# The f16 halves of x go through a DMA transpose, and GpSimd's constant-operand copies become tensor-scalar operations

## The chip, the cores and the metric

One core of a Trainium2 chip runs the kernel. The metric is the device time of one execution in microseconds (us); lower is better. Engines are named as the profile names them: PE is TensorE's matmul side and PEld its weight loads, DVE is VectorE, ACT is ScalarE, POOL is GpSimd, SP is SyncE, whose instruction queue issues nearly all DMA transfers here (SPq in the profile).

## What is computed

A decoder layer over 32 sequences of 128 tokens with 256 channels, 16 heads of width 16: linear attention with random features, cross attention, a ternary gated feed-forward; a layer norm stands behind each. Cut to its core:

```python
q, k, v = (split(x @ W.T + b) for W, b in ((Wq, bq), (Wk, bk), (Wv, bv)))
q_phi, k_phi = phi(q), phi(k)          # phi(y) = exp(y @ orf.T / dk**.25 - |y|^2 / (2 dk**.5)) + eps
kv = einsum('bhlm,bhld->bhmd', k_phi, v)
att = einsum('bhlm,bhmd->bhld', q_phi, kv) / einsum('bhlm,bhm->bhl', q_phi, k_phi.sum(2))[..., None]
x = layernorm(x + merge(att) @ Wo.T + bo)
s = softmax((x_heads @ xWq.T) @ (ctx_heads @ xWk.T).T / 4) @ (ctx_heads @ xWv.T)
x = layernorm(x + merge(s))
h = silu(quant(x) @ tern(w_gate).T) * (quant(x) @ tern(w_up).T)
out = layernorm(x + quant(h) @ tern(w_down).T)
```

In the cross attention x gives the queries, the context keys and values. `quant` rounds to 8-bit levels per token, `tern` rounds weights to -1, 0, 1.

## The kernel before

One tile is one sequence: 128 tokens on the partitions, 256 channels along them. A tile's work is cut into some 110 named steps, and all engines run a software pipeline written out by hand: each engine has a function `iteration(i, par)` that lists its steps in a fixed order, and `go(step, i, par, lag)` runs the step on tile i - lag. So in iteration i TensorE projects tile i - 1, makes features of tile i - 3, scores of tile i - 6, the feed-forward of tiles i - 8 and i - 9. Iterations 0 to 13 are written out, 14 to 31 are a loop of two iterations a pass, and 32 to 41 are written out again and drain the pipeline. Each step raises a semaphore (`done[name]`, for transposes by DMA `moved[name][par]`), and `wait(eng, name, t, off)` waits for it. An engine does its steps in order, so a waiting step holds all behind it.

Around the change:

- x of a tile is loaded by SP (`load_x`, L286) into `xs`. POOL makes its f16 half `xhi` (L394) by a multiplication with a tensor of ones, and the rest `xlo` (L401), both into the single buffer `xpk`.
- `xTp` (L1070) on TensorE transposes `xpk` in 4 blocks of 128x128 into bank 6, late in iteration t, between `st0` and `st1`. `xT_` (L539) on ScalarE copies them to `xT`, as the last step of its iteration. `qkm` (L1088) in iteration t + 1 reads `xT` first, right behind `s0`; `vm` reads it again later.
- SP's list in an iteration (L338) is `load_c`, `load_x`, `cT_`, `kT`, `hqT_`, `qT`, `row`, `tT_`, `load_r`, `store`. `cT_`, `kT`, `hqT_`, `qT` and `tT_` are DMA transposes of [128, 1024] in f16 or bf16, all issued at L305 and waited for in `wait_ahead` (L242). `tT_` waits for `tlo` of DVE (L857), `row` for `mT` of ACT (L612), `hqT_` for `hq0` of POOL, `kT` for `lo` of POOL.
- The hidden layer comes quantised through `hs` (DVE) - `hm1`, `hm0` (ACT) - `hq1`, `hq0` (POOL, L469 to L477, an addition of a broadcast constant) - `hqT_` (SP, DMA) - `dn` (TensorE, L1293). Behind `dn` in TensorE's list stand `vm`, `tm`, `kvp`, `wo`, `st0`.
- `tm` (L1177) - `thi` (ACT, L602) - `tlo` (DVE) - `tT_` (SP): the query side of the scores. DVE does `kvm_` and `ad3` ahead of `tlo`.
- POOL's other operations with a constant operand: `chi` (L449, context, 512 elements a partition), `xqf` (L463, 256).

Of the kernel before, what the change touches and what calls it, by code (L numbers as in the profile page):

```python
# [12 lines left out]
P = 128  # L13
# [17 lines left out]
def decoder_kernel(nc: bass.Bass, x, ctx_in, Wq, bq, Wk, bk, Wv, bv, Wo, bo, orf,  # L31
# [4 lines left out]
    with ExitStack() as stack:  # L36
# [6 lines left out]
        def sem(name):  # L43
# [54 lines left out]
        xT = sb("xT", [P, 4, P], F16)  # L98
# [96 lines left out]
        at_xT = pb[6][:, 0:256]  # L195
# [30 lines left out]
        moved = {name: [sem(f"s_{name}{i}") for i in range(2)] for name in ("qT", "kT", "cT", "tT", "hqT", "row")}  # L226
# [15 lines left out]
        def wait_ahead(eng, t, *producers):  # L242


            counts = [t + off + 1 for _, off in producers]
            counts = [v if isinstance(v, int) else eng.to_reg(v) for v in counts]
            eng.wait_ge(ids, 3)
            for (name, _), v in zip(producers, counts):
                if not isinstance(v, int) or v > 0:
                    eng.wait_ge(done[name], v)  # L250
# [27 lines left out]
        def _(sp):  # L278
# [27 lines left out]

            def qT(t, par):

                wait_ahead(sp, t, ("phq0", -1))
                transpose(pkAT[:, 0:PAIRS, :], pkA[:, 0:PAIRS, :, :].rearrange("p c r d -> p (c r d)"), "qT", par)  # L310
# [27 lines left out]
            def iteration(i, par):  # L338
                go(load_c, i, par, 4)
                go(load_x, i, par, 0)  # L340
                go(cT_, i, par, 5)
                go(kT, i, par, 2)
                go(hqT_, i, par, 9)
                go(qT, i, par, 2)
                go(row, i, par, 6)
                go(tT_, i, par, 5)
                go(load_r, i, par, 3)
                go(store, i, par, 10)
# [6 lines left out]
        def _(pool):  # L355
# [38 lines left out]
            def xhi(t, par):  # L394

                landed(pool, x_in, t, par)
                wait(pool, "xTp", t, -1)
                g.tensor_tensor(xpk[:, 0, :], xs[:, par, :], onesf[:, 0:1].to_broadcast([P, D]),
                                ALU.mult).then_inc(done["xhi"], 1)
# [49 lines left out]
            def chi(t, par):  # L449

                landed(pool, c_in, t, par)
                wait_moved(pool, "cT", t, par, -1)
                c3 = cs[:, par, :].rearrange("p (h d) -> p h d", h=H)
                g.tensor_tensor(pkC[:, :, 0:2, :], c3.unsqueeze(2).to_broadcast([P, H, 2, DK]),
                                onesf[:, 0:1].unsqueeze(2).unsqueeze(3).to_broadcast([P, H, 2, DK]),
                                ALU.mult).then_inc(done["chi"], 1)
# [6 lines left out]
            def xqf(t, par):  # L463

                wait(pool, "qnt", t)
                g.tensor_tensor(xq[:, par, :], xm[:, par, :], nmagic[:, :].to_broadcast([P, D]),  # L466
                                ALU.add).then_inc(done["xqf"], 1)

            def hq0(t, par):  # L469
                wait(pool, "hm0", t)  # L470
                g.tensor_tensor(hq[:, 0, :], hm[:, 0, :], nmagic[:, :].to_broadcast([P, 512]),
                                ALU.add).then_inc(done["hq0"], 1)

            def hq1(t, par):
                wait(pool, "hm1", t)
                g.tensor_tensor(hq[:, 1, :], hm[:, 1, :], nmagic[:, :].to_broadcast([P, 512]),  # L476
                                ALU.add).then_inc(done["hq1"], 1)  # L477
# [20 lines left out]
        def _(act):  # L498
# [39 lines left out]

            def xT_(t, par):  # L539
                wait(act, "xTp", t)  # L540
                copy(xT[:, :, :], at_xT.bitcast(F16).rearrange("p (c t) -> p c t", c=4), "xT")
# [116 lines left out]
            def iteration(i, par):  # L658
# [22 lines left out]
                go(xT_, i, par, 0)  # L681
# [338 lines left out]
        def _(pe):  # L1020
# [49 lines left out]
            def xTp(t, par):  # L1070
                wait(pe, "xlo", t)
                wait(pe, "ad3", t, -9)
                dst = at_xT.bitcast(F16)
                for k in range(4):
                    last = T.transpose(dst[:, k * P:(k + 1) * P], xpk[:, k // 2, (k % 2) * P:(k % 2 + 1) * P],
                                       idh[:, :])
                last.then_inc(done["xTp"], 1)

            def project(o, cols, name):

                n = 0
                for c in range(2):
                    for part, w in ((0, wq_hi), (0, wq_lo), (1, wq_hi)):
                        last = T.matmul(o, xT[:, 2 * part + c, :], w[:, c, cols], start=(n == 0), stop=(n == 5))  # L1084
                        n += 1
                last.then_inc(done[name], 1)

            def qkm(t, par):  # L1088
                wait(pe, "xT", t)
                project(at_qk, slice(0, 2 * D), "qkm")  # L1090

            def vm(t, par):
# [3 lines left out]
                project(at_v, slice(2 * D, 3 * D), "vm")  # L1096
# [15 lines left out]
            def phq1(t, par):  # L1112
                wait_moved(pe, "qT", t, par)
                wait(pe, "xT", t, 2)
                features_q(at_phq1, 1, "phq1")
# [184 lines left out]
            def iteration(i, par):  # L1300
# [26 lines left out]
                go(xTp, i, par, 0)  # L1327
# [26 lines left out]
```

## Time and profile before

| | us |
|---|---|
| median of 3 runs | 568.69 |
| lowest, highest | 567.56, 572.29 |
| the profiled execution | 565.91 |
| its span, from first to last instruction | 564.2 |

| engine | busy us | share of span |
|---|---|---|
| PE | 486.1 | 86% |
| DVE | 472.4 | 84% |
| ACT | 411.2 | 73% |
| POOL | 387.6 | 69% |

The profile is of one execution. A busy share is a mean over filling, full and draining pipeline, so the stretch with the full pipeline is to be read by itself. A row of the order-of-time view gives start, duration, engine, line and operation; what stands in square brackets is the idle time ahead of it on its engine and what ended that. For SPq the duration is that of the issue; a transfer's landing is given separately, counted from the start of its issue.

### The profile page before, as it was taken

The numbers are of one execution on the slowest core, as the hardware profiler recorded it, in microseconds if no ns is written. First come the engines' busy times: TensorE is split into PE (matmuls) and PEld (weight loads), VectorE is DVE, ScalarE is ACT, GpSimd is POOL, SyncE is SP. The second block draws the span as 40 slices with busy tenths as digits, with TensorE's granted clock in tenths as the row PEclk, the third lists the DMA queues.
The fourth block names the chain that finished last, engine by engine and source line by source line (L and its number), as shares of the span: only waits on it lengthen the run. The fifth ranks groups of instructions, "written<-read, shape, count | busy, mean of one in ns | idle before, by whom it ended". The sixth has DMA issues, their size and how long they took to land.

```text
span 564.2 us, 17426 instructions
## 1 busy us (share of the span) xinstructions
PE 486.1 (86%) x5932; PEld 345.5 (61%) x5990; DVE 472.4 (84%) x1380; ACT 411.2 (73%) x811; POOL 387.6 (69%) x768
## 2 busy tenths in 40 slices
PE   3056999999999998999999999999999998977651
PEld 2034766677667676777777777777777776654320
DVE  0784565889999998999999999999999998998671
ACT  0226667778888887888888888888888887867531
POOL 7032665677777777788777777788788876665432
PEclk9576999999999999999999999999999999998765
DMA  5604776566877775556565656566555587473111
GB/s 142 221 0 82 138 133 110 87 122 122 135 131 133 132 125 110 125 124 131 117 130 120 130 118 130 119 129 124 121 125 123 124 124 122 87 113 67 41 45 37
DMA packets 192649, 64.14 MB, mean 114 GB/s; under 512 B 172384, under 2 KB 192352, under 8 KB 192608
## 3 DMA queue, kind: packets, MB, share of 16 engines
q1 hardware_dynamic: 190080, 60.46, 55.3%
q10 hardware_dynamic: 2528, 3.15, 1.7%
q8 instruction: 24, 0.39, 0.3%
q14 instruction: 17, 0.14, 0.1%
HBM read 17.31 MB, written 4.19 MB: 38 GB/s over the span
## 4 chain that ended last, share of the span: by engine, by line
PE 60%; DVE 12%; DMA 9%; ACT 7%; issue 4%; SPq 4%; POOL 4%; ACTq 0%; POOLq 0%; DVEq 0%
PE bank L1084 9%; PE bank L1151 8%; PE bank L1274 5%; DMA hqT<-hq 5%; PE bank L1244 5%; PE bank L1297 4%; PE bank L1167 3%; PE bank L1104 3%; PE bank L1149 3%; PE bank L1133 2%; PE bank L1099 2%; PE bank L1181 2%; PE bank L1261 2%; DMA tT<-nmT 2%; PE bank L1224 1%
## 5 line engine op out<-in xcount | busy, mean ns | idle before, releaser
L1084 PE MATMUL bank<-wq_hi,xT 128*128 128x512 f16 (+1 forms) x256 | 71.7, 336 | 0.9 <-ACT xT L511 0.7
L1151 PEld LDWEIGHTS bank<-kvm,phq 128*128 128x128 f32 x512 | 62.2, 192 | 2.5
L1151 PE MATMUL bank<-kvm,phq 128*128 128x34 f32 x512 | 59.8, 272 | 0.0
L416 POOL TENSOR_TENSOR pkA<-qk,pkA 128x512 f16<-128x512 f32 x32 | 37.6, 1176 | 31.7 <-ACT pkA L511 31.6
L466 POOL TENSOR_TENSOR xq<-xm,nmagic 128x256 bf16<-128x256 f32 x32 | 19.6, 613 | 51.5 <-DVE xm L911 51.5
L430 POOL TENSOR_TENSOR rs<-ve,mhalf 128x1 f32<-128x1 f32 x96 | 52.9, 552 | 0.0
L865 DVE TENSOR_REDUCE negm<-bank 128x4 f16<-128x512 f32 x64 | 43.8, 685 | 8.6 <-PE bank L1200 8.5
L555 ACT ACTIVATE x<-y,nmr,rs 128x256 f32<-128x256 f32 x64 | 38.3, 599 | 11.1 <-DVE y L976 9.7
L915 DVE SCALAR_TENSOR_TENSOR g<-th,bank 128x512 f32<-128x512 f32 x64 | 43.2, 676 | 3.7 <-ACT th L643 3.6
L1244 PE MATMUL bank<-pT,ctxv 128*32 128x128 f32 x1024 | 42.4, 284 | 4.5 <-ACT pT L620 4.3
L511 ACT ACTIVATE pkT<-bank 128x512 f16<-128x512 f32 x32 | 19.1, 597 | 37.0 <-PE bank L1181 37.0
L1297 PE MATMUL bank<-downT,hqT 128*128 128x256 bf16 x256 | 34.6, 280 | 12.8 <-DMA hqT<-hq 12.8
L866 DVE TENSOR_REDUCE negm<-bank 128x4 f16<-128x512 f32 x64 | 43.5, 680 | 0.0
L922 DVE TENSOR_REDUCE hmax<-hh 128x1 f32<-128x512 f32 x64 | 43.2, 676 | 0.0
L1084 PE MATMUL bank<-wq_lo,xT 128*128 128x256 f16 (+1 forms) x128 | 42.8, 334 | 0.0
L576 ACT ACTIVATE phq<-bank 128x512 f32<-128x512 f32 x64 | 38.0, 593 | 5.7 <-PE bank L1099 5.7
L576 ACT ACTIVATE phk<-bank 128x512 f32<-128x512 f32 x64 | 39.4, 622 | 3.2 <-PE bank L1104 3.2
L919 DVE TENSOR_TENSOR hh<-g,bank 128x512 f32<-128x512 f32 x64 | 40.9, 679 | 0.0
L619 ACT ACTIVATE pT<-bank 128x512 f32<-128x512 f32 x64 | 37.6, 588 | 4.1 <-PE bank L1225 4.1
L1297 PEld LDWEIGHTS bank<-downT,hqT 128*128 128x128 bf16 x256 | 24.2, 100 | 26.4 <-DMA hqT<-hq 18.2
L476 POOL TENSOR_TENSOR hq<-hm,nmagic 128x512 bf16<-128x512 f32 x32 | 33.3, 1042 | 8.4 <-ACT hm L655 8.4
L837 DVE BATCH_NORM_STATS2 st<-y 128x6 f32<-128x256 f32 x96 | 38.7, 403 | 0.0
(180 smaller groups left out, 1611.5 us busy)
## 6 DMA issues: line engine op xcount, KB each, us to landing
xs<-in_x_dram SPq DMA_DIRECT2D x32, 128.0 KB, 2.5
xr<-in_x_dram SPq DMA_DIRECT2D x32, 128.0 KB, 2.2
cs<-in_ctx_dram SPq DMA_DIRECT2D x32, 128.0 KB, 2.2
out_dram<-ot SPq DMA_DIRECT2D x32, 128.0 KB, 1.9
ffn_ld<-in_L_ffn_w_gate_dram ACTq DMA_DIRECT2D x1, 1024.0 KB, 5.5
ffn_ld<-in_L_ffn_w_up_dram ACTq DMA_DIRECT2D x1, 1024.0 KB, 8.7
ffn_ld<-in_L_ffn_w_down_dram ACTq DMA_DIRECT2D x1, 1024.0 KB, 10.5
pkAT<-pkA SPq DMA_TRANSPOSE x64, 3.2
```

What stands on the lines that cost most here:

```text
L430: g.tensor_tensor(rs[n - 1][:, :], ve[n - 1][:, :], mhalf[:, :], ALU.pow).then_inc(done[f"pw{n}"], 1)
L576: sc.activation(o, i.rearrange("p (c t) -> p c t", c=parts), ACT.Exp, scale=0.5).then_inc(done[name], 1)
L837: v.bn_stats(st[n - 1][:, :], y[n - 1][:, par, :]).then_inc(done[f"stats{n}"], 1)
L865: v.tensor_reduce(negm[:, 0, cols], even.rearrange("p (c t) -> p c t", c=4), AX, ALU.max, negate=True)
L866: v.tensor_reduce(negm[:, 1, cols], odd.rearrange("p (c t) -> p c t", c=4), AX, ALU.max, negate=True).then_inc(done[name], 1)
L915: v.scalar_tensor_tensor(g1[:, n, :], th[:, n, :], 1.0, gate, ALU.add, ALU.mult).then_inc(done[f"gl{n}"], 1)
L919: v.tensor_tensor(hh[:, n, :], g1[:, n, :], up, ALU.mult).then_inc(done[f"hu{n}"], 1)
L922: v.tensor_reduce(hmax2[:, n:n + 1], hh[:, n, :], AX, ALU.max, apply_absolute_value=True).then_inc(done[f"hh{n}"], 1)
L1084: last = T.matmul(o, xT[:, 2 * part + c, :], w[:, c, cols], start=(n == 0), stop=(n == 5))
L1151: last = T.matmul(at_num[:, 2 * DV * k:2 * DV * (k + 1)], phq[:, par, k, :], kvm[:, k, :, :].rearrange("p h d -> p (h d)"), start=False, s ...
L1244: last = T.matmul(at_pv[32 * j:32 * j + 32, q * P:(q + 1) * P], ctxv[:, par, h, :], pT[:, grp, odd, k, :], start=True, stop=True)
L1297: last = T.matmul(at_dn, hqT[:, k, :], downT[:, k, :], start=(k == 0), stop=(k == 7))
```

## The change

The steps `xTp` (TensorE) and `xT_` (ScalarE) are dropped, with their places in the lists. `xT` becomes double buffered, and a new step `xT_` on SP fills it by one DMA transpose of [128, 512] in f16; it stands between `tT_` and `load_r` in SP's list, for the tile of lag 0. It waits for `xlo` of its tile and for `vm` of the tile two before. `qkm` waits for the transfer, and gets the two waits (`qk` of the tile before, `p0` at -6) that `xTp` and `xT` had implied. On POOL `xhi`, `chi`, `xqf`, `hq0` and `hq1` become `tensor_scalar` operations with two immediate numbers instead of `tensor_tensor` with a broadcast tensor, and their waits are written with `wait_ahead`, which computes the register values before it waits.

```diff
@@ -95,7 +95,7 @@
         xs = sb("xs", [P, 2, D])
         xr = sb("xr", [P, 2, D])
         xpk = sb("xpk", [P, 2, D], F16)
-        xT = sb("xT", [P, 4, P], F16)
+        xT = sb("xT", [P, 2, 4, P], F16)
         qk = sb("qk", [P, 2 * H, DK])
         vv = sb("vv", [P, 2, H, 32])
         qk2 = sb("qk2", [P, 2 * H, DK])
@@ -192,7 +192,6 @@
         at_phq1 = pb[6][:, :]
         at_aT = pb[6][:, 0:256]
         at_dn = pb[6][:, 0:256]
-        at_xT = pb[6][:, 0:256]
         at_qk = pb[7][:, :]
         at_x1T = pb[7][:, 0:256]
         at_st0b = pb[7][:, :]
@@ -214,7 +213,7 @@
         x_in, r_in, c_in, stored = ([sem(f"{n}{i}") for i in range(2)] for n in ("x_in", "r_in", "c_in", "stored"))
 
         done = {name: sem("s_" + name) for name in (
-            "xhi xlo xb xTp xT qkm vm qk v sq nf nr nhi nlo hi lo phq0 phq1 ephq0 ephq1 phk0 phk1 ephk0 "
+            "xhi xlo xb qkm vm qk v sq nf nr nhi nlo hi lo phq0 phq1 ephq0 ephq1 phk0 phk1 ephk0 "
             "ephk1 kvs vsm kve kvp kvm nump rd at aTp aT wo ad1 y1 rs1 x1 chi clo vhp vh x1Tp x1T tm "
             "thi tlo s0 s1 m0 m1 mTp mT st0 st1 p0 p1 pv0 pv1 oxT oxp rx oxn ya2 y2 rs2 x2 am ac ar sg "
             "qnt xqf xqTp xqT g0 u0 g1 u1 th0 th1 gl0 hu0 hh0 gl1 hu1 hh1 hx hc hr sd hs hm0 hm1 hq0 "
@@ -223,7 +222,7 @@
         ).split()}
 
 
-        moved = {name: [sem(f"s_{name}{i}") for i in range(2)] for name in ("qT", "kT", "cT", "tT", "hqT", "row")}
+        moved = {name: [sem(f"s_{name}{i}") for i in range(2)] for name in ("qT", "kT", "cT", "tT", "hqT", "row", "xT")}
 
         def wait_moved(eng, name, t, par, off=0):
 
@@ -239,12 +238,16 @@
             if not isinstance(v, int) or v > 0:
                 eng.wait_ge(done[name], v)
 
-        def wait_ahead(eng, t, *producers):
+        def wait_ahead(eng, t, *producers, queues=()):
 
 
             counts = [t + off + 1 for _, off in producers]
             counts = [v if isinstance(v, int) else eng.to_reg(v) for v in counts]
+            bytes_in = [v if isinstance(v, int) else eng.to_reg(v) for _, v in queues]
             eng.wait_ge(ids, 3)
+            for (semaphore, _), v in zip(queues, bytes_in):
+                if not isinstance(v, int) or v > 0:
+                    eng.wait_ge(semaphore, v)
             for (name, _), v in zip(producers, counts):
                 if not isinstance(v, int) or v > 0:
                     eng.wait_ge(done[name], v)
@@ -304,6 +307,11 @@
             def transpose(o, i, name, par):
                 sp.dma_start_transpose(o, i).then_inc(moved[name][par], 16)
 
+            def xT_(t, par):
+
+                wait_ahead(sp, t, ("xlo", 0), ("vm", -2))
+                transpose(xT[:, par, :, :], xpk[:, :, :].rearrange("p n d -> p (n d)"), "xT", par)
+
             def qT(t, par):
 
                 wait_ahead(sp, t, ("phq0", -1))
@@ -344,6 +352,7 @@
                 go(qT, i, par, 2)
                 go(row, i, par, 6)
                 go(tT_, i, par, 5)
+                go(xT_, i, par, 0)
                 go(load_r, i, par, 3)
                 go(store, i, par, 10)
             run(sp, iteration)
@@ -393,10 +402,10 @@
 
             def xhi(t, par):
 
-                landed(pool, x_in, t, par)
-                wait(pool, "xTp", t, -1)
-                g.tensor_tensor(xpk[:, 0, :], xs[:, par, :], onesf[:, 0:1].to_broadcast([P, D]),
-                                ALU.mult).then_inc(done["xhi"], 1)
+                before = (par - 1) % 2
+                wait_ahead(pool, t, queues=((x_in[par], t * 8 - par * 8 + 16),
+                                            (moved["xT"][before], (t - 1 - before) * 8 + 16)))
+                g.tensor_scalar(xpk[:, 0, :], xs[:, par, :], 1.0, 0.0, ALU.mult, ALU.add).then_inc(done["xhi"], 1)
 
             def xlo(t, par):
                 wait(pool, "xhi", t)
@@ -448,12 +457,12 @@
 
             def chi(t, par):
 
-                landed(pool, c_in, t, par)
-                wait_moved(pool, "cT", t, par, -1)
+                before = (par - 1) % 2
+                wait_ahead(pool, t, queues=((c_in[par], t * 8 - par * 8 + 16),
+                                            (moved["cT"][before], (t - 1 - before) * 8 + 16)))
                 c3 = cs[:, par, :].rearrange("p (h d) -> p h d", h=H)
-                g.tensor_tensor(pkC[:, :, 0:2, :], c3.unsqueeze(2).to_broadcast([P, H, 2, DK]),
-                                onesf[:, 0:1].unsqueeze(2).unsqueeze(3).to_broadcast([P, H, 2, DK]),
-                                ALU.mult).then_inc(done["chi"], 1)
+                g.tensor_scalar(pkC[:, :, 0:2, :], c3.unsqueeze(2).to_broadcast([P, H, 2, DK]), 1.0, 0.0,
+                                ALU.mult, ALU.add).then_inc(done["chi"], 1)
 
             def clo(t, par):
                 wait(pool, "chi", t)
@@ -462,19 +471,16 @@
 
             def xqf(t, par):
 
-                wait(pool, "qnt", t)
-                g.tensor_tensor(xq[:, par, :], xm[:, par, :], nmagic[:, :].to_broadcast([P, D]),
-                                ALU.add).then_inc(done["xqf"], 1)
+                wait_ahead(pool, t, ("qnt", 0))
+                g.tensor_scalar(xq[:, par, :], xm[:, par, :], 1.0, -MAGIC, ALU.mult, ALU.add).then_inc(done["xqf"], 1)
 
             def hq0(t, par):
-                wait(pool, "hm0", t)
-                g.tensor_tensor(hq[:, 0, :], hm[:, 0, :], nmagic[:, :].to_broadcast([P, 512]),
-                                ALU.add).then_inc(done["hq0"], 1)
+                wait_ahead(pool, t, ("hm0", 0))
+                g.tensor_scalar(hq[:, 0, :], hm[:, 0, :], 1.0, -MAGIC, ALU.mult, ALU.add).then_inc(done["hq0"], 1)
 
             def hq1(t, par):
-                wait(pool, "hm1", t)
-                g.tensor_tensor(hq[:, 1, :], hm[:, 1, :], nmagic[:, :].to_broadcast([P, 512]),
-                                ALU.add).then_inc(done["hq1"], 1)
+                wait_ahead(pool, t, ("hm1", 0))
+                g.tensor_scalar(hq[:, 1, :], hm[:, 1, :], 1.0, -MAGIC, ALU.mult, ALU.add).then_inc(done["hq1"], 1)
 
             def iteration(i, par):
                 go(xqf, i, par, 8)
@@ -535,10 +541,6 @@
 
             def evacuate_rest():
                 evacuate_ffn((2, 3, 4, 5))
-
-            def xT_(t, par):
-                wait(act, "xTp", t)
-                copy(xT[:, :, :], at_xT.bitcast(F16).rearrange("p (c t) -> p c t", c=4), "xT")
 
             def sq(t, par):
                 wait(act, "qk", t)
@@ -678,7 +680,6 @@
                 go(x2_, i, par, 7)
                 go(p0, i, par, 6)
                 go(p1, i, par, 6)
-                go(xT_, i, par, 0)
             run(act, iteration, between={1: (evacuate_gate,), 2: (evacuate_rest,)})
 
 
@@ -1067,33 +1068,26 @@
 
             orf_pair = orfp[:, :, :].rearrange("p h m -> p (h m)")
 
-            def xTp(t, par):
-                wait(pe, "xlo", t)
-                wait(pe, "ad3", t, -9)
-                dst = at_xT.bitcast(F16)
-                for k in range(4):
-                    last = T.transpose(dst[:, k * P:(k + 1) * P], xpk[:, k // 2, (k % 2) * P:(k % 2 + 1) * P],
-                                       idh[:, :])
-                last.then_inc(done["xTp"], 1)
-
-            def project(o, cols, name):
+            def project(o, cols, par, name):
 
                 n = 0
                 for c in range(2):
                     for part, w in ((0, wq_hi), (0, wq_lo), (1, wq_hi)):
-                        last = T.matmul(o, xT[:, 2 * part + c, :], w[:, c, cols], start=(n == 0), stop=(n == 5))
+                        last = T.matmul(o, xT[:, par, 2 * part + c, :], w[:, c, cols], start=(n == 0), stop=(n == 5))
                         n += 1
                 last.then_inc(done[name], 1)
 
             def qkm(t, par):
-                wait(pe, "xT", t)
-                project(at_qk, slice(0, 2 * D), "qkm")
+                wait_moved(pe, "xT", t, par)
+                wait(pe, "qk", t, -1)
+                wait(pe, "p0", t, -6)
+                project(at_qk, slice(0, 2 * D), par, "qkm")
 
             def vm(t, par):
                 wait(pe, "vh", t, -5)
                 wait(pe, "ephq0", t, -2)
                 wait(pe, "v", t, -1)
-                project(at_v, slice(2 * D, 3 * D), "vm")
+                project(at_v, slice(2 * D, 3 * D), par, "vm")
 
             def features_q(o, n, name):
                 T.matmul(o, orf_pair, pkAT[:, 4 * n:4 * n + 4, :].rearrange("p c t -> p (c t)"),
@@ -1111,7 +1105,7 @@
 
             def phq1(t, par):
                 wait_moved(pe, "qT", t, par)
-                wait(pe, "xT", t, 2)
+                wait(pe, "ad3", t, -7)
                 features_q(at_phq1, 1, "phq1")
 
             def phk0(t, par):
@@ -1324,7 +1318,6 @@
                 go(kvp, i, par, 3)
                 go(wo, i, par, 4)
                 go(st0, i, par, 6)
-                go(xTp, i, par, 0)
                 go(st1, i, par, 6)
                 go(nump, i, par, 3)
             run(pe, iteration, between={0: (ffn_means,), 1: (transpose_gate,), 2: (transpose_rest,)})
```

## Rows read from the trace of the kernel before

**Rows 1.** The chain that ended last, full pipeline, two iterations apart: start us, us, what.
```profile
304.17 0.33 PE bank L1075 x4
...
318.74 0.33 PE bank L1075 x4
```

**Rows 2.** A stretch: its us, busy PE, PEld, DVE, ACT, POOL, PEclk, DMA share, GB/s.
```profile
152.18:460.96 308.78, 302.17 (x3844) 218.21 (x3886) 290.86 (x882) 261.20 (x525) 245.85 (x483) 1.00 0.63 125
```

**Rows 3.** SP's issues in order of time, iteration A (behind the loop's branch).
```profile
304.37 1.25 SPq L305 DMA_TRANSPOSE tT<-pkT  x1
...
308.07 0.34 SPq L288 DMA_DIRECT2D xs<-in_x_dram  x1
...
310.08 1.23 SPq L305 DMA_TRANSPOSE pkAT<-pkA  x1
311.48 1.25 SPq L305 DMA_TRANSPOSE hqT<-hq  x1
...
318.95 1.25 SPq L305 DMA_TRANSPOSE tT<-pkT  x1
```

**Rows 4.** The same, iteration B (the loop's other half).
```profile
260.66 1.26 SPq L305 DMA_TRANSPOSE tT<-pkT  x1
...
265.87 1.26 SPq L305 DMA_TRANSPOSE pkAT<-pkA  x1
267.64 1.24 SPq L305 DMA_TRANSPOSE hqT<-hq  x1
```

**Rows 5.** POOL in order of time: hq0 of an iteration B and of A.
```profile
266.51 1.04 POOL L471 TENSOR_TENSOR hq<-hm,nmagic 128x512 bf16<-128x512 f32 x1
...
310.22 1.04 POOL L471 TENSOR_TENSOR hq<-hm,nmagic 128x512 bf16<-128x512 f32 x1
```

**Rows 6.** Instructions and landings of hqT, 150 to 430 us (forms behind the dash).
```profile
L305 SPq DMA_TRANSPOSE hqT<-hq x19: 1231/1242/1272, 162.8 to 428.1; - x19
...
DMA to landing us min/median/max: 3.2/3.3/4.8
```

**Rows 7.** PE in order of time: dn free of waiting, and one that waited.
```profile
315.19 1.04 PE L1297 MATMUL bank<-downT,hqT 128*128 128x256 bf16 x8
...
167.44 1.05 PE L1297 MATMUL bank<-downT,hqT 128*128 128x256 bf16 x8 [0.52 <-DMA hqT<-hq]
```

**Rows 8.** SP at 162 to 171 us, and the landing of the first of them.
```profile
162.80 1.23 SPq L305 DMA_TRANSPOSE hqT<-hq  x1
...
171.08 1.25 SPq L305 DMA_TRANSPOSE tT<-pkT  x1
...
DMA to landing us min/median/max: 4.6/4.6/4.6
```

**Rows 9.** Waits, 150 to 430 us: total us, times, longest.
```profile
PEld bank L1297 <- DMA hqT<-hq: 4.7, 5, 1.9
...
SPq L250 <- DVE pkT L859: 36.0, 19, 3.2
```

**Rows 10.** PE in order of time: the first matmul of qkm in an iteration A.
```profile
309.48 0.39 PE L1084 MATMUL bank<-wq_hi,xT 128*128 128x512 f16 x1
```

**Rows 11.** POOL in order of time: a one-input and a no-input operation.
```profile
2.44 0.95 POOL L363 MEMSET pkC<- 128x1024 f16 x1
...
8.83 0.60 POOL L382 TENSOR_SCALAR_AFFINE_SELECT kvmask<-kvmask 128x272 f32<-128x272 f32 x1
```

**Rows 12.** The chain that ended last, filling pipeline.
```profile
45.67 0.48 ACT xT L511
...
83.49 0.33 PE bank L1075 x4
```

**Rows 13.** The same, draining pipeline.
```profile
541.87 0.61 POOL xq L466
...
543.43 1.05 POOL hq L471
...
552.73 1.05 POOL hq L471
```

## The prediction, made before the changed kernel was run

> **What bounds the kernel now.** I read the page's busy shares first (86% PE, 84% DVE), which say little, since they average over filling and draining. The busy times of a full stretch say more: between the start of dn in one iteration and 21 iterations later PE is busy 302.17 of 308.78 us, DVE 290.86, ACT 261.20, POOL 245.85 [rows 2]. Then the chain that ended last: in the full pipeline it runs through PE alone, and the four transposes of xTp stand in it with 0.33 us, 14.57 us apart [rows 1]. So PE sets the iteration at 14.57 us, and 308.78 us is 21 x 14.57 = 306.0 and 2.8 us of stalls. DVE's own work is 290.86 / 21 = 13.85 us an iteration.
>
> Then I looked for what is nearly as long as PE's round, because a step is taken from PE and given to SP. SP's issues in order of time show it. In an iteration A (just behind the loop's branch) tT is issued at 304.37, and from there SP issues without a pause worth the name until hqT at 311.48, 7.11 us later; kT ends at 310.08 + 1.23 = 311.31, so hqT is held by the queue, not by hq0, which ended at 311.26 [rows 3, 5]. In the other half of the loop, B, kT ends at 265.87 + 1.26 = 267.13, while hq0 ends at 266.51 + 1.04 = 267.55 and hqT goes at 267.64: there POOL holds it, 6.98 us behind tT; the queue alone would have let it go 0.17 us behind kT, at 267.30, which is 6.64 us [rows 4, 5]. hqT lands 3.3 us after its issue (median, 4.8 at most) [rows 6]. In A that is 314.78, and dn starts at 315.19 [rows 3, 7]: 0.4 us of room.
>
> This closes a ring: tT issued - queue - hqT issued - landing - dn - vm - tm - thi - tlo - tT of the next iteration. Its last piece is to be read where dn did wait: hqT issued at 162.80 and landed 4.6 us later, at 167.40; dn starts at 167.44 and the next tT goes at 171.08, 3.64 us behind it [rows 7, 8]. Without a wait the ring takes
>
> - A: 7.11 + 3.3 + 0.04 + 3.64 = 14.09 us
> - B: 6.98 + 3.3 + 0.04 + 3.64 = 13.96 us (6.64, so 13.62, by the queue alone)
>
> against PE's 14.57. It hides, with half a microsecond to spare.
>
> **The change, part by part.**
>
> *xTp gone from PE:* 4 transposes, 0.33 us an iteration in the chain [rows 1]. PE's round becomes 14.57 - 0.33 = 14.24 us.
>
> *xT_ gone from ACT:* its place in the chain was 0.48 us [rows 12]. ACT has 308.78 - 261.20 = 47.6 us idle in 21 iterations [rows 2], so in the full pipeline this gives only that hi, hm1, hm0 come earlier, and with them hq0. That takes away B's wait on POOL, nothing else: the queue holds hqT.
>
> *xT_ on SP:* one more transpose, half as wide, between tT and load_r, so inside the ring. SP has time for it: it waits 36.0 us in 19 iterations for tlo alone, 1.9 us each [rows 9]. But that wait is on the other side of tT; every issue between tT and hqT comes later by the whole price. Queued behind it are load_r, store, load_c, load_x, cT, kT, hqT and qT. The loads and cT, kT, qT are read an iteration later; only hqT is awaited at once, by dn, and behind dn stand vm, tm and the rest of the ring.
>
> Its issue price is not in the trace. A transpose of [128, 1024] takes 1.23 to 1.27 us to issue [rows 3, 6], a plain load of 128 rows 0.34 [rows 3]. From below it is bounded by half, 0.62, if the price goes with the width (0.34 if a narrow transpose were as cheap as a load), from above by 1.25 if it does not go with the width. A line through the load's 128 rows at 0.34 and 1024 transposed columns at 1.25 gives 0.73 for 512. I take 0.73, since a width-bound cost with a small fixed part fits both rows. To this comes the gap between two issues, 0.11 to 0.2 us; kT to hqT shows 0.17 [rows 3]; I take 0.16. So 0.89 us, bounds 0.5 and 1.45.
>
> The ring then takes: A 14.09 + 0.89 = 14.98, B 13.62 + 0.89 = 14.51. Both are over PE's 14.24, so the ring is the bound. Mean 14.74, against 14.57: +0.17 us an iteration. It counts from iteration 8 (first hqT in 9) to 31: 24 x 0.17 = **+4.1 us**. With 0.5 us it would be A 14.59, B 14.24 (PE), mean 14.42: 24 x -0.15 = -3.7. With 1.45: A 15.54, B 15.07, mean 15.31: 24 x 0.74 = +17.7.
>
> *Late landings:* hqT landed over 3.3 us in some early iterations of the loop, 5 of 19 with a wait of 4.7 us at PEld [rows 9]. Before, PE's slack took a part: all stalls are 2.8 us. In a kernel bound by the ring each costs in full. Between 4.7 - 2.8 = 1.9 and 1: **+1.5 us**.
>
> *Does qkm wait for xT?* xT is issued 1.25 + 0.16 = 1.41 us behind tT and its issue ends at 2.14. A load lands some 2 us behind the end of its issue, hqT 3.3 - 1.24 = 2.1 behind; so xT lands about 4.2 us behind tT. qkm begins 309.48 - 304.37 = 5.1 us behind tT [rows 3, 10], 4.8 without xTp in between. Hidden, with 0.6 us; at an issue of 1.25 it lands at 4.8, just in time.
>
> The Trainium skill speaks against such a move: in "VectorE: DVE Perf Modes", section on the three transpose paths, it gives a 128x128 transpose 390 ns on TensorE and 1309 ns by DMA, and its rules say to use TensorE where PSUM will do. As an estimate from that page four blocks by DMA would be 5.2 us, against 1.24 us of issue for eight blocks in this trace; the trace does not bear that out as a sum over blocks. What the rule would do here is a rival below.
>
> *POOL's operations:* hq0 and hq1 take 1.04 us each (512 elements), xqf 0.61 (256) [rows 5, 13]. One-input operations in the trace: a memset of 1024 in 0.95 us, so 0.48 for 512; an affine select of 272 in 0.60, so 1.13 for 512 [rows 11]. I take 0.65 for 512 and 0.4 for 256, between them and nearer the memset, because the new form is plain arithmetic on one stream. In the full pipeline it is hidden behind SP's queue (POOL idles 63 us of 308.78 [rows 2]). In the drain POOL is on the chain: xqf once and hq1, hq0 in two iterations [rows 13]: 0.2 + 4 x 0.4 = **-1.8 us**; bounds -2.5 and +0.4.
>
> The page "GPSIMD Engine Reference", section 4.1, of the Trainium skill calls one-input work roughly line rate and two-input work twice as slow as VectorE. By its 1.03 cycles an element at 1.2 GHz, as an estimate, 512 elements would be 0.44 us, and the drain would give -2.6.
>
> *Filling:* iterations 0 to 8 are not in the ring. The chain passes ACT's xT once (0.48) and xTp four times, one with 0.22 and three with 0.33, of which one is shown [rows 12]: -1.7. In iteration 6 s0 follows tT's landing at once, and xT lands behind it: +0.3. **-1.4 us**. The start is set by weight preparation, and x's first load and halves are not in its way.
>
> **Sum:** 4.1 + 1.5 - 1.8 - 1.4 = +2.4 us on the profiled execution's 565.91 = 568.3. The median of the runs is 568.69 - 565.91 = 2.8 above that execution, so 571.
>
> **The rivals.**
>
> *Slower, the issue does not shrink with the width.* SP pays 1.25 us for 512 columns too. The ring without xT is 13.86 us in the mean of A and B, the other terms are 1.5 - 1.8 - 1.4 = -1.7, so the result is over 1% slower (5.7 us) when 24 x (ring - 14.57) is over 7.4: from a ring of 14.88 on, which is an issue of 0.86 us. At 1.25: 13.86 + 1.41 = 15.27, 24 x 0.70 = 16.8, less 1.7 is +15: **584**. For it: 64 issues of this kind and one width only, so nothing shows a slope. Against it: plain loads of different sizes differ.
>
> *Faster, the ring does not bind.* If the narrow transpose issues in 0.34 like a load and hqT lands a few tenths sooner, PE's 14.24 shows: 24 x -0.33 = -7.9, with -1.8 - 1.4: -11: **558**. For it: the ring's pieces are read to 0.05 us, but the landing's range is 1.6 us wide. Against it: in A the queue is full and there is 0.4 us of room only.
>
> *Slower, the transfer is late for qkm.* This is what the skill's rule would mean here. If xT took 4.8 us to land (the longest landing of hqT [rows 6]) each time, a second ring closes: 1.41 + 4.8 + from qkm to dn 315.19 - 309.48 = 5.7 + 3.64 = 15.55, +0.98 an iteration over 31 iterations: +30.4, less 3.2 from filling and draining, +27: **596**. Against it: the landings of a transfer twice as wide are 3.3.
>
> **How the numbers follow.** The likeliest case is the ring with an issue of 0.6 to 0.95 us: 571, own range 568 to 577 (24 x 0.05 and 24 x 0.40, less 1.7). Chances: this case 0.60, the slower issue 0.20, PE's round 0.15, late xT 0.05. About 1%, 5.7 us, is what a measurement can tell from no change. Part of the first case (0.11) lies over that on the slow side, and 0.02 on the fast side: faster 0.17, same 0.47, slower 0.36. The range leaves out late xT and the outermost of the two others: 559 to 584.
>
> **What would show it.** SP issues xT in 0.6 to 0.95 us (rival: 1.25). hqT goes about 8.0 us behind tT in A and 7.5 in B, and SP never waits for hq0 any more. dn waits for hqT in nearly every iteration, and the period of dn is 15.0 and 14.5 in turn. PE's busy time in 21 iterations is 7 us less and its idle time 10 us more. qkm does not wait for xT. POOL's hq0 takes about 0.65 us. I am wrong if dn waits seldom and the period is under 14.5, or if something other than hqT ends PE's idle time: then the ring was not closed as I drew it, or a landing moved.

## The result, and the profile after

| | us |
|---|---|
| kernel before, median of 4 runs | 569.44 |
| changed kernel, median of 4 runs | 585.28 (583.4 to 589.54) |
| ratio | 1.0284, 95% interval 1.0211 to 1.0358 |

The changed kernel is 2.8% slower. The forecast was 571 with a range of 559 to 584. The measured time lies 1.3 us above the upper end, and the case called the likeliest did not happen: the time is close to what the first rival gave, 584. The profiled execution of the changed kernel took 589.54 us, the longest of its four, and that of the kernel before 565.91, less than any of its four, so the rows of the two show a larger loss (23.6 us) than the medians do (15.8).

The chain that ended last shows where the time went. These are its shares by engine and by line, from the page of the changed kernel. Before, PE had 60% of it and SPq 4%.

```profile
SPq 32%; DMA 23%; PE 18%; DVE 10%; issue 9%; ACT 5%; POOL 1%; ACTq 0%; DVEq 0%; POOLq 0%
SPq L308 23%; DMA hqT<-hq 16%; PE bank L1291 5%; PE bank L1076 4%; SPq L295 2%; DMA xs<-in_x_dram 2%; DMA ffn_ld<-in_L_ffn_w_down_dram 2%; PE bank L1175 2%; DMA tT<-nmT 2%; SPq L299 2%; DVE pkT L860 2%; SPq L291 2%; SPq L303 2%; PE bank L1238 1%; PE bank L1145 1%
```

L308 is where all transposes by DMA are issued. Next, SP's issues in order of time in the changed kernel: start, duration, what. The iteration that begins at 304.61 is a B, the one at 319.47 an A. They answer to [rows 3, 4].

```profile
304.61 1.25 SPq L308 DMA_TRANSPOSE tT<-pkT  x1
306.05 1.20 SPq L308 DMA_TRANSPOSE xT<-xpk  x1
...
311.04 1.26 SPq L308 DMA_TRANSPOSE pkAT<-pkA  x1
312.47 1.25 SPq L308 DMA_TRANSPOSE hqT<-hq  x1
...
319.47 1.25 SPq L308 DMA_TRANSPOSE tT<-pkT  x1
320.92 1.20 SPq L308 DMA_TRANSPOSE xT<-xpk  x1
...
328.13 1.26 SPq L308 DMA_TRANSPOSE hqT<-hq  x1
```

xT, half as wide as tT, takes 1.20 us to issue against 1.25. hqT goes 312.47 - 304.61 = 7.86 us behind tT in B and 8.66 in A. Before it was 6.98 and 7.11. Then dn on PE, in order of time, with the idle time ahead of it [rows 7]:

```profile
285.34 1.05 PE L1291 MATMUL bank<-downT,hqT 128*128 128x256 bf16 x8 [0.58 <-DMA hqT<-hq]
300.97 1.05 PE L1291 MATMUL bank<-downT,hqT 128*128 128x256 bf16 x8 [1.31 <-DMA hqT<-hq]
315.83 1.05 PE L1291 MATMUL bank<-downT,hqT 128*128 128x256 bf16 x8 [0.55 <-DMA hqT<-hq]
```

dn now waits in every iteration of the loop; the period is 15.63 and 14.86 in turn, 15.24 in the mean, against 14.57. The busy times from 240 to 440 us (columns as in [rows 2]) show PE idle for 12.2 of 200 us, 6%. In the same stretch of the kernel before it was idle for 2.8 us.

```profile
240.00:440.00 200.00, 187.80 (x2371) 133.28 (x2370) 180.47 (x548) 155.50 (x312) 133.30 (x302) 1.00 0.62 128
```

The waits from 150 to 430 us, of PE first and then of SP's queue (total us, times, longest). They answer to [rows 9]: SP no longer waits for hq0 at all, and hqT has become the largest wait of PE.

```profile
PE bank L1291 <- DMA hqT<-hq: 22.4, 18, 2.3
...
SPq L253 <- DVE pkT L860: 52.1, 18, 5.1
```

The landings in the same stretch, from the views of hqT and of xT, against [rows 6]: hqT's median is what it was, its longest went from 4.8 to 5.4 us.

```profile
DMA to landing us min/median/max: 3.2/3.3/5.4
...
DMA to landing us min/median/max: 2.4/2.4/2.5
```

### The profile page after: what moved, and what is told of

It reads as the page before. It is cut to its first block, busy times and chain, and to the rows that moved or that the text cites. A ratio compares the mean times of both kernels' runs of the same rounds, so it can differ in the third digit from the quotient of the medians.

```text
span 587.7 us, 17359 instructions
## 1 busy us (share of the span) xinstructions
PE 486.8 (83%) x5862; PEld 338.7 (58%) x5862; DVE 472.4 (80%) x1380; ACT 394.9 (67%) x779; POOL 337.5 (57%) x768
## 4 chain that ended last, share of the span: by engine, by line
SPq 32%; DMA 23%; PE 18%; DVE 10%; issue 9%; ACT 5%; POOL 1%; ACTq 0%; DVEq 0%; POOLq 0%
SPq L308 23%; DMA hqT<-hq 16%; PE bank L1291 5%; PE bank L1076 4%; SPq L295 2%; DMA xs<-in_x_dram 2%; DMA ffn_ld<-in_L_ffn_w_down_dram 2%; PE bank L1175 2%; DMA tT<-nmT 2%; SPq L299 2%; DVE pkT L860 2%; SPq L291 2%; SPq L303 2%; PE bank L1238 1%; PE bank L1145 1%
## 5 line engine op out<-in xcount | busy, mean ns | idle before, releaser
L1076 PE MATMUL bank<-wq_hi,xT 128*128 128x512 f16 (+1 forms) x256 | 73.3, 342 | 1.0 <-DMA xT<-xpk 0.8
L475 POOL TENSOR_SCALAR xq<-xm 128x256 bf16<-128x256 f32 x32 | 13.3, 417 | 96.1 <-DVE xm L912 96.1
L429 POOL TENSOR_TENSOR y<-ox,x 128x256 f32<-128x256 f32 x32 | 23.3, 730 | 33.2 <-DVE ox L887 33.0
L1268 PE MATMUL bank<-gateT,xqT 128*128 128x512 bf16 x128 | 40.5, 407 | 1.4 <-DVE negm L867 0.9
## 6 DMA issues: line engine op xcount, KB each, us to landing
ffn_ld<-in_L_ffn_w_down_dram ACTq DMA_DIRECT2D x1, 1024.0 KB, 12.2
```

The source lines that it names most:

```text
L1076: last = T.matmul(o, xT[:, par, 2 * part + c, :], w[:, c, cols], start=(n == 0), stop=(n == 5))
```

## Experiments

The theory: SP's queue is part of a ring (tT - queue - hqT - landing - dn - vm - tm - thi - tlo - tT), and what is issued between tT and hqT lengthens it by its issue time. The rivals: the bytes of xT in the shared DMA engines delay hqT; qkm waits for xT; POOL's new operations slow something.

### xT moved out of the ring

```diff
                 go(row, i, par, 6)
-                go(tT_, i, par, 5)
                 go(xT_, i, par, 0)
+                go(tT_, i, par, 5)
```

> The changed kernel with SP's xT step moved one place, ahead of tT, so out of the stretch between tT and hqT and into SP's wait for tlo. Same transfers, same bytes. Theory (queue in the ring): hqT goes about 7.1 us behind tT in A and 6.6 to 7.0 in B again, dn waits seldom, the period falls from 15.3 to PE's 14.2 to 14.3 us, time 557 to 562. Rival (the DMA engines are shared by more bytes, so hqT lands later wherever xT stands): about 585, as the changed kernel. Rival (xT lands too late for qkm): no change in place would help, qkm would wait.

Measured: 560.04 us, ratio to the kernel before 0.9853 (0.9794 to 0.9912). One line changes place and 25 us go. SP in order of time, and dn:

```profile
303.98 1.20 SPq L308 DMA_TRANSPOSE xT<-xpk  x1
305.61 1.24 SPq L308 DMA_TRANSPOSE tT<-pkT  x1
...
312.86 1.24 SPq L308 DMA_TRANSPOSE hqT<-hq  x1
...
287.71 1.05 PE L1291 MATMUL bank<-downT,hqT 128*128 128x256 bf16 x8
301.86 1.04 PE L1291 MATMUL bank<-downT,hqT 128*128 128x256 bf16 x8
316.12 1.05 PE L1291 MATMUL bank<-downT,hqT 128*128 128x256 bf16 x8
```

xT fits into the time in which SP had waited for tlo. tT to hqT is 7.25 us, the period (316.12 - 287.71) / 2 = 14.2 us. The same bytes flow, qkm depends on the same transfer and POOL does the same work, yet the loss is gone, so none of these three is the cause. The ring is not quite hidden, though. From 240 to 440 us PE is still idle for 3.5 us, and its weight loads for dn wait for hqT 8 times, 4.2 us in all:

```profile
240.00:440.00 200.00, 196.46 (x2509) 142.24 (x2536) 191.70 (x589) 167.86 (x337) 143.20 (x326) 1.00 0.66 138
```

### hqT issued first

```diff
                 go(load_x, i, par, 0)
+                go(hqT_, i, par, 9)
                 go(cT_, i, par, 5)
                 go(kT, i, par, 2)
-                go(hqT_, i, par, 9)
```

> The changed kernel with xT where the change put it, but hqT issued ahead of cT and kT. The stretch from tT to hqT still holds xT (1.2 us) but loses two issues of 1.25 us. Theory (queue in the ring): ring about 15.3 - 2 x 1.4 = 12.5 us, below PE's 14.24, so dn does not wait and the time is 557 to 562, the same as with xT moved. Rival (bytes): hqT would land a little earlier by its place, but the DMA engines carry the same; about 580. What could spoil it: hq0 ends about 5.7 us behind tT, so SP waits for it for some 0.7 us with cT and kT behind it; both are read an iteration later.

Measured: 563.05 us, ratio 0.9906 (0.9868 to 0.9944), 1 us above the expected range. xT stands where the change put it, yet the loss is gone, since the stretch lost two other issues. The ten executions scatter from 559.13 to 567.54 us. In the profiled one, which is the slowest, SP waits 10.1 us in all for hq0, and PE 5.5 us for the row, which is issued behind it.

### An extra transpose in the kernel before

```diff
                 go(tT_, i, par, 5)
+                go(extra, i, par, 0)
                 go(load_r, i, par, 3)
```

`extra` is a DMA transpose of a [128, 512] f16 tensor of zeros into a spare double buffer that no engine waits for.

> The kernel before, with everything on TensorE and POOL as it was, plus a transpose by DMA of 128x512 f16 zeros into a spare buffer that nobody waits for, at SP's place between tT and load_r. Theory (queue in the ring): ring 14.09 + 1.36 = 15.45 in A and 13.62 + 1.36 = 14.98 in B, both over PE's 14.57; mean 15.2, 24 x 0.65 = +15.5 and late landings +1.5: 585 to 588, as slow as the changed kernel although its 0.33 us of PE work is there too. Rival (the slowdown comes from the wait of qkm for xT or from POOL's new operations): 569 to 571.

Measured: 587.0 us, ratio 1.0319 (1.0253 to 1.0385). SP and dn:

```profile
303.31 1.25 SPq L308 DMA_TRANSPOSE tT<-pkT  x1
304.75 1.20 SPq L316 DMA_TRANSPOSE spare<-idle  x1
...
311.20 1.25 SPq L308 DMA_TRANSPOSE hqT<-hq  x1
...
284.04 1.05 PE L1310 MATMUL bank<-downT,hqT 128*128 128x256 bf16 x8
299.67 1.05 PE L1310 MATMUL bank<-downT,hqT 128*128 128x256 bf16 x8 [0.89 <-DMA hqT<-hq]
314.53 1.05 PE L1310 MATMUL bank<-downT,hqT 128*128 128x256 bf16 x8
```

The period is (314.53 - 284.04) / 2 = 15.25 us, the changed kernel's, with xTp still on PE. So PE's 0.33 us are worth nothing once the ring binds. This reproduces the whole loss by one issue that nobody waits for.

### The price of an issue by itself

```diff
                 sp.wait_ge(stored[par], 16 * TILES // 2)
+            flat = pkC[:, :, :, :].rearrange("p h r d -> p (h r d)")
+            n = 0
+            for again in range(2):
+                for parts, cols in ((128, 128), (128, 256), (128, 512), (128, 1024), (64, 512), (32, 512)):
+                    sp.dma_start_transpose(probe[:, 0:cols // 128, 0:parts], flat[0:parts, 0:cols]).then_inc(probed, 16)
+                    n += 1
+                    sp.wait_ge(probed, 16 * n)
```

> The changed kernel, with 12 transposes by DMA at SP's very end, one at a time, each waited for: 128x128, 128x256, 128x512, 128x1024, 64x512, 32x512 (partitions x columns), twice. It prices the disputed issue alone. Theory A (the issue goes with the width, a small fixed part): 0.45, 0.55, 0.73, 1.25 us. Theory B (what the changed kernel's 1.20 for 512 against 1.25 for 1024 says: fixed): 1.15 to 1.25 for all widths. For partitions nothing is known: if the issue goes with them, 64 and 32 rows are cheaper. The tail adds some 40 us to the time, which says nothing.

Measured, SP in order of time, the first six in the order of the list (the second six agree within 0.01 us):

```profile
590.75 1.13 SPq L367 DMA_TRANSPOSE probe<-pkC  x1
593.01 1.18 SPq L367 DMA_TRANSPOSE probe<-pkC  x1
595.32 1.19 SPq L367 DMA_TRANSPOSE probe<-pkC  x1
597.75 1.23 SPq L367 DMA_TRANSPOSE probe<-pkC  x1
600.81 1.17 SPq L367 DMA_TRANSPOSE probe<-pkC  x1
603.11 1.16 SPq L367 DMA_TRANSPOSE probe<-pkC  x1
```

1, 2, 4 and 8 blocks cost 1.13, 1.18, 1.19 and 1.23 us of SP's time; a half or a quarter of the partitions 1.17 and 1.16. The price is per instruction, with at most 0.1 us for the width.

### The same bytes as a plain copy, and a quarter of the bytes as a transpose

Two doses at the place of `extra` in the kernel before:

```diff
-                sp.dma_start_transpose(spare[:, par, :, :], idle[:, :])
+                sp.dma_start(spare[:, par, :, :], idle[:, :].rearrange("p (c t) -> p c t", c=4))
```

> The kernel before with an extra transfer at the same place as in the run with the extra transpose, and of the same 128 KB, but a plain copy from SBUF to SBUF, which should take 0.35 to 0.45 us to issue instead of 1.20. Theory (the issue's time on SP's queue): ring 14.09 + 0.55 = 14.64 in A, 14.17 in B, PE 14.57: at most +1 us and some late landings, 569 to 572. Rival (the bytes in the DMA engines delay hqT): 585 to 588, as with the transpose.

```diff
-                sp.dma_start_transpose(spare[:, par, :, :], idle[:, :])
+                sp.dma_start_transpose(spare[:, par, 0:1, :], idle[:, 0:P])
```

> The same again with a transpose of one block, 128x128, a quarter of the bytes. It took 1.13 us to issue at the end of the queue. Theory (price per instruction): ring + 1.13 + 0.16 = 15.38 in A, 14.91 in B, mean 15.15, 24 x 0.58 = +13.9 and late landings +1.5: 583 to 586. Rival (bytes): a quarter of +16, 573.

| in the ring, kernel before | issue us | KB | period us | time us | ratio |
|---|---|---|---|---|---|
| nothing | 0 | 0 | 14.57 | 568.3 | 1 |
| plain copy 128x512 | 0.54 | 128 | 14.86 | 576.25 | 1.0136 (1.0107 to 1.0164) |
| transpose 128x128 | 1.12 | 32 | 15.23 | 587.9 | 1.0318 (1.0274 to 1.0363) |
| transpose 128x512 | 1.20 | 128 | 15.25 | 587.0 | 1.0319 (1.0253 to 1.0385) |

The time follows the issue and not the bytes: a quarter of the bytes costs as much as all of them. The transpose of one block is 2 us over its expected 583 to 586. The plain copy cost more than expected, 8 us and not 1. Its rows show why, SP first and then dn:

```profile
279.18 1.24 SPq L308 DMA_TRANSPOSE tT<-pkT  x1
280.61 0.54 SPq L316 DMA_DIRECT2D spare<-idle  x1
...
287.20 1.27 SPq L308 DMA_TRANSPOSE hqT<-hq  x1
...
275.42 1.04 PE L1310 MATMUL bank<-downT,hqT 128*128 128x256 bf16 x8
290.55 1.05 PE L1310 MATMUL bank<-downT,hqT 128*128 128x256 bf16 x8 [0.39 <-DMA hqT<-hq]
305.13 1.04 PE L1310 MATMUL bank<-downT,hqT 128*128 128x256 bf16 x8
```

tT to hqT is 8.02 us in A, 0.91 more than before: 0.54 of issue and 0.37 in gaps around it, where I had allowed 0.55 for both. A's ring is then 8.02 + 3.3 + 0.04 + 3.64 = 15.00, and its period 15.13; B keeps PE's 14.58. With either transpose both are longer, 15.6 in A and 14.85 in B. As an estimate from this sum, 14.57 - 14.09 - 0.37 = 0.1: hardly any further issue fits into A for nothing.

### POOL's part alone, and the transpose alone

The first is the kernel before with the `tensor_scalar` forms of the change, the second the changed kernel with the `tensor_tensor` forms of before; the diff of both is the POOL part of the change, once done and once undone.

> The kernel before with the POOL part of the change alone (xhi, chi, xqf, hq0, hq1 as tensor-scalar); transposes stay on TensorE. Theory: hidden in the full pipeline behind PE, on the chain in the drain for 0.2 + 4 x 0.42 us, so -2 us, 566 to 568. It would also end B's wait of SP for hq0. Rival (POOL's reads slow DVE, so fewer of them speed it up all along): 560 or less.

> The changed kernel with POOL's operations as before, so the DMA transpose alone. Theory: the ring is SP's and holds no POOL work, so the loss is the changed kernel's: its time plus the 2 us of the drain, 586 to 589. If hq0, 0.8 us later than in the changed kernel, came to hold hqT, it would be more: hq0 ended 5.7 us behind tT there, hqT goes at 7.9, so there is room. Rival (POOL's new operations cause part of the slowdown): under 580.

Measured: POOL alone 564.58 us, ratio 0.9941 (0.9918 to 0.9964); the transpose alone 587.32, ratio 1.032 (1.0269 to 1.037). The second is the ratio of the run with the extra transpose (1.0319), although here xTp and xT_ are gone from PE and ACT: while the ring binds, taking them away gives nothing. POOL's part is a small gain, 3.7 us where 2 were expected, and below the expected 566 to 568. In its profiled execution the last dn of the full pipeline starts at 460.61 and the span ends at 561.7, 101.1 us later, against 103.2 before: 2.1 us in the drain.

### Can more of the ring be opened?

Three more orders of SP's list. First both moves together, xT ahead of tT and hqT first, in the changed kernel:

> The changed kernel with both moves: xT ahead of tT, and hqT ahead of cT and kT. Theory: with xT moved alone the period is already PE's 14.2 us from 240 us on; what is left of the ring are the late landings early in the loop, where PE waited 4.5 us in all for hqT. With hqT 2.8 us earlier they are hidden: 556 to 558. Rival (nothing left to gain, or SP's wait for hq0 now holds cT and kT): 559 to 562.

Measured: 561.69 us, ratio 0.9884 (0.9855 to 0.9912); 556 to 558 was expected. That is the rival's 559 to 562, and its condition is in the trace: from 150 to 430 us SP waits for hq0 31.0 us, in 18 iterations. Then hqT first (the diff shown above) in the kernel before, and nothing else:

> The kernel before with hqT ahead of cT and kT and nothing else. It asks whether the ring was hidden in the kernel before. Theory: yes, PE's 14.57 us set it; hqT is then held by hq0 (6.9 us behind tT) and comes hardly earlier, so only a part of the 2.8 us of stalls goes: 566 to 569. Rival (the ring was already the bound, PE only looked busy): 555 to 562.

Measured: 591.2 us, ratio 1.0362 (1.031 to 1.0415), where at most a small gain was expected. This was my largest miss. The chain of that kernel, in order of time (start, us, what):

```profile
297.43 1.06 POOL hq L471
...
298.56 1.25 SPq L305
...
302.80 1.29 SPq L305
...
304.14 0.68 SPq L331
...
304.88 1.67 DMA tT<-nmT
...
306.59 0.23 PE bank L1224
...
327.88 1.04 POOL hq L471
```

A second ring: hqT waits for hq0 (SP 63.4 us in 18 iterations), and behind it stand cT, kT, qT (298.56 to 304.09 are hqT's issue and theirs) and then row, which st0 on PE awaits; from there PE, DVE and POOL lead back to hq0. The chain passes SP once between these two hq0, and SP issues two hqT in that time: one round of 327.88 - 297.43 = 30.45 us spans two iterations, 15.2 us for each. In the kernel before hqT stood behind cT and kT, so that their issues ran while hq0 was not yet there. POOL's operations are part of this second ring, and with the faster ones it is shorter; that would be why hqT first did no harm in the changed kernel and much here. The changed kernel also has no xTp on PE, and no run separates the two.

So the next run keeps the order of the transposes of the run with xT moved, and takes only the load and the store out of the stretch:

```diff
                 go(hqT_, i, par, 9)
                 go(qT, i, par, 2)
+                go(load_r, i, par, 3)
+                go(store, i, par, 11)
                 go(row, i, par, 6)
+                go(xT_, i, par, 0)
                 go(tT_, i, par, 5)
-                go(xT_, i, par, 0)
-                go(load_r, i, par, 3)
-                go(store, i, par, 10)
-            run(sp, iteration)
+            run(sp, iteration, lags=11)
```

> The changed kernel with xT ahead of tT, and load_r and the store (one iteration later) taken out of the stretch from tT to hqT: they stand behind qT. The order of the transposes is as in the run with xT moved alone, so the ring that opened when hqT stood first (hq0 - hqT - cT - kT - qT - row - st0) stays closed off. Theory: hqT goes some 1.3 us earlier behind tT than with xT moved alone, which hides most of the 4.5 us that PE waited for late landings early in the loop: 557 to 559, against 560. Rival 1 (the row is now later by 1.2 us of issues and PE waits at st0): 562 to 570. Rival 2 (those late landings cost nothing at the end): 560, no difference.

Measured: 553.76 us, ratio 0.9757 (0.9718 to 0.9796): 2.4% faster than the kernel before, the best of all, and 3 us under the expected 557 to 559. PE is busy without a pause from 240 to 440 us, and the period is 14.14 us (columns as in [rows 2], then dn):

```profile
240.00:440.00 200.00, 200.00 (x2554) 143.95 (x2551) 192.60 (x594) 169.53 (x342) 143.75 (x328) 1.00 0.67 140
...
255.22 1.04 PE L1291 MATMUL bank<-downT,hqT 128*128 128x256 bf16 x8
269.36 1.04 PE L1291 MATMUL bank<-downT,hqT 128*128 128x256 bf16 x8
283.50 1.04 PE L1291 MATMUL bank<-downT,hqT 128*128 128x256 bf16 x8
```

The expectation put the gain over the run with xT moved alone into late landings early in the loop. The dn rows of the two profiled executions (562.01 and 556.28 us) divide it otherwise: 2.3 us up to the first dn, 1.5 over the next eight iterations, 1.7 over the fifteen behind them, where the period fell from 14.26 to 14.14, and 0.3 in the drain. So with xT moved alone the ring still held PE a little, and PE's own round is 14.14 us. The 2.3 us of filling are not explained.

In the same chip's session, xT moved ahead of tT in the kernel with the transpose alone, so with POOL as before:

> The run with xT ahead of tT, with POOL's operations as before. It shares the gain out. Theory: POOL's part is worth the 3.7 us that it gave alone, mostly in the drain, and the transpose off TensorE the rest: 563 to 565. Should POOL's old, 0.8 us slower hq0 hold hqT in B as it did in the kernel before, the ring there is 13.96, under PE's 14.24: no more than that. Rival (POOL's part is worth more once PE is faster, since DVE and POOL are closer to being the bound): 566 to 569.

Measured: 561.18 us, ratio 0.9887 (0.9851 to 0.9923), 2 us under the expected 563 to 565. With POOL's part as well the ratio was 0.9853, and the two intervals overlap, so what POOL's part adds here (about 0.3%) is not told from nothing. So the transpose by DMA by itself gains about 1.1% at a place outside the ring, and costs 3.2% at the place where the change put it.

## Why the prediction was wrong, point by point

**What bounds the kernel: right.** PE set 14.57 us, and the ring of tT, hqT and dn lay just below. The extra transpose, which closes the ring without touching anything else, shows it. The terms held too: landing 3.3, and with 7.86 and 8.66 the ring gives 14.84 and 15.64 us, against the measured 14.86 and 15.63. PE's own round was put at 14.24 and is 14.14 us, as the run with the loads behind hqT shows: without xTp it lost 0.43 and not 0.33 us. While the ring binds, this changes nothing.

**The issue price of the narrow transpose: wrong, and it is the step that failed.** The prediction put a line through a plain load of 128 rows (0.34 us) and a transpose of 1024 columns (1.25) and took 0.73 for 512. The trace had one width of transpose only, and the load is another operation; the line joined two things that share no slope. Measured: 1.20 in the kernel, 1.13 to 1.23 over a factor of eight in width. With 1.20 the same sum reads 13.86 + 1.36 = 15.22 us, 24 x 0.65 = 15.6, less 1.7: +13.9, so 582.6, within the range; the 2.7 us that are left to the measured 585.28 lie in the smaller terms below. This is the first rival, to which 20% was given. The row that should have weighed more was the one at hand: five kinds of transposes (160 issues in the trace, where the prediction counts 64) at 1.23 to 1.28 said nothing of a slope, and the bound of 1.25 deserved as much as 0.73.

**The gaps: a little low in sum.** 0.16 us was taken. The stretch grew in B from its queue-only 6.64 to 7.86, by 1.22, and in A from 7.11 to 8.66, by 1.55; the mean, 1.39, is 1.20 of issue and 0.19 of gaps.

**Late landings: right in kind, too small.** From the first dn to the one 23 iterations later the profiled executions took 338.4 us before (122.53 to 460.96) and 359.0 after (125.49 to 484.47): +20.5. The ring's mean accounts for 23 x 0.67 = 15.4, so some 5 us lie in the slow iterations early in the loop, against 1.5 predicted. The changed kernel's profiled execution is the longest of its four, so the median's share is smaller, and how much smaller is open.

**Filling: not confirmed.** -1.4 us was predicted; the first dn started at 125.49 instead of 122.53, +3.0. In the profiled executions of the other kernels with xT on SP it was between -0.3 (xT moved, POOL as before) and +3.5 (xT moved); with the changed kernel's own order and POOL as before it was +0.9. None shows the -1.4, and no +3.0 that belongs to the transpose. In the changed kernel the chain passes through SP: in an early iteration xT stands behind kT and qT, which wait for a pipeline not yet full, and the next load of x stands behind xT. The prediction weighed what xT needs and not who stands behind it in these iterations. This is read from one execution and was not tried by itself.

**Draining:** POOL's operations took 0.62 us for 512 elements and 0.40 for 256 (0.65 and 0.4 predicted), and alone they shortened the drain by 2.1 us (1.8 predicted). In the changed kernel's profiled execution the stretch from that same dn to the end is 103.2 us, as before. With the transpose alone it is 105.7 us (479.20 to 584.9), so POOL's part took 2.5 us off here too, and the transpose put 2.5 on, a term that the prediction does not have. What lengthens the drain is open, and these are single executions. The prediction's estimate from the page's rate (-2.6) leaves out what the same rate gives for xqf; with it it is -2.8.

**qkm and xT: right.** xT lands 2.4 us after the start of its issue, so 3.8 behind tT (4.2 predicted), and qkm waits for it in no iteration of the full pipeline. With it falls the rival of the late xT, beside which a page was named. The Trainium skill's page "VectorE: DVE Perf Modes" would have kept the transposes on TensorE. The time of the changed kernel goes that way, but by the queue's issue and not by a late landing, and with xT issued at another place the kernel is faster with them on the DMA queue (1.1% by themselves).

**B's wait for hq0: right,** it is gone.

## What to carry to other kernels

In this kernel the instruction queue that only issues transfers had a place in a dependency ring as an engine has. So look for the pair of issues that bound the stretch (here tT and hqT), and put new issues into the part of the round where the queue waits. SP had 1.9 us of waiting in each iteration, and whether the new 1.2 us fell behind tT or ahead of it, into that waiting, decided between 2.8% slower and 1.5% faster. Where an unknown price has two rows on either side that are of different kinds, measure it alone or give the ends equal weight; and when an issue is moved forward past others, ask what it waits for, because those behind it then wait too.

## What the runs showed of the hardware

A DMA transpose costs SP 1.13 us for one block and 1.23 for eight, and 1.16 to 1.17 with 32 or 64 partitions; a plain copy of 128 rows between SBUF tensors costs 0.54. As an estimate from these, the same eight blocks as two transposes of four (2 x 1.19) would cost SP nearly twice what one of eight does.

hqT's landings go with the transfers of instructions (queues q8 and q14). From the DMA view of the changed kernel, first 150 to 235 us, then 240 to 450 (where no instruction queue is listed); the last number is the median landing in us:

```profile
q8 instruction: 8, 0.13, 0.8%
q14 instruction: 6, 0.05, 0.2%
...
hqT<-hq SPq DMA_TRANSPOSE x5, 4.6
...
hqT<-hq SPq DMA_TRANSPOSE x13, 3.3
```

In the kernel before it is 4.2 and 3.3, and there it can be followed transfer by transfer. Of 27 hqT from 118 to 498 us, 9 have an instruction transfer in the 4 us behind the start of their issue: they land after 3.0 to 5.0 us, seven of them after 3.8 or more. The other 18 all land after 3.1 to 3.4. In the changed kernel two hqT without such a transfer were late too (5.4 and 3.9 us, issued at 152.67 and 493.93, and their issues took 2.49 and 1.92 us). That the one causes the other is likely by the times, but no run here takes the instruction transfers away.

POOL's `tensor_scalar` with two immediates takes 0.62 us for 512 elements a partition and 0.40 for 256, where `tensor_tensor` with a broadcast operand took 1.04 and 0.61. For each further element that is 0.86 ns against 1.68. The Trainium skill, "GPSIMD Engine Reference", section 4.1, calls one-input work roughly line rate and two-input work about twice as slow as on VectorE. That one input is the cheaper form agrees with it; no run here puts the same operation on VectorE.
